# Inverse roots in the second edge stage: three Newton steps on VectorE in place of ScalarE's square root and a reciprocal

## What is computed

```
def _inst_norm_lastdim(t):
    mu = jnp.mean(t, axis=-1, keepdims=True)
    var = jnp.mean(jnp.square(t - mu), axis=-1, keepdims=True)
    return (t - mu) * jax.lax.rsqrt(var + EPS)
qkv = jnp.einsum('bnc,fc->bnf', x, Wqkv)        # 8 heads of 64
k = _inst_norm_lastdim(k)
v = _inst_norm_lastdim(v)
dots = jnp.einsum('bhnd,bhne->bhde', k, v)
out = jnp.einsum('bhnd,bhde->bhne', q, dots) / n
```

## Time and profile before

| | |
|---|---|
| median of 3 runs | 1760.73 us |
| lowest and highest | 1758.09 and 1762.08 us |
| the profiled execution | 1765.67 us, its span 1763.9 us |
| busy, share of the span | PE 77%, DVE 53%, POOL 54%, ACT 35% |
| TensorE's mean granted clock | 0.868 of full speed |
| second edge stage, first to last product | 798.2 to 1538.9 us |

### The profile page before, as it was taken

One profiled execution on the slowest core, in us unless ns is written; L12 is line 12 of the kernel. 1 busy time (PEld: TensorE's weight loads), 2 busy tenths in 40 slices (PEclk: granted clock), 3 DMA queues, 4 the chain that ended last, 5 costly groups with the idle time before them and its releaser, 6 DMA issues.

```text
span 1763.9 us, 39415 instructions
## 1 busy us (share of the span) xinstructions
PE 1350.7 (77%) x13431; PEld 801.7 (45%) x13431; DVE 935.0 (53%) x2353; ACT 616.5 (35%) x1897; POOL 957.8 (54%) x1008
## 2 busy tenths in 40 slices
PE   3668778877788775657778787888887878856999
PEld 1345454554455444343444444444444444543458
DVE  4445555454433343655555555555555556676763
ACT  2233333333333332243343433334343433323420
POOL 0677777777777774016665666666566656500000
PEclk9699988988988898778888888888888888977999
DMA  6333333333333330323333333333333333300001
GB/s 199 96 81 75 81 81 75 76 86 75 87 75 82 75 85 20 134 69 100 92 102 89 101 89 93 91 96 93 94 91 89 97 90 103 85 24 1 1 10 38
DMA packets 78954, 141.94 MB, mean 80 GB/s; under 512 B 25483, under 2 KB 34091, under 8 KB 78249
## 3 DMA queue, kind: packets, MB, share of 16 engines
q0 software_dynamic: 40128, 81.99, 17.8%
q1 hardware_dynamic: 38632, 57.46, 10.9%
HBM read 134.69 MB, written 4.67 MB: 79 GB/s over the span
## 4 chain that ended last, share of the span: by engine, by line
PE 44%; POOL 16%; issue 15%; DVE 12%; ACT 5%; DMA 5%; DVEq 2%; SPq 1%; ACTq 0%; POOLq 0%; PEldq 0%
POOL ring L412 16%; PE ps L932 8%; PE ps L946 8%; DVE arena L1357 5%; PE ps L919 5%; DMA ring<-mtab,src 4%; PE ps L968 4%; PE ps L1093 3%; PE ps L1084 3%; PE ps L762 2%; DVE arena L1355 2%; ACT wfT L583 1%; PE ps L694 1%; DVE arena L1347 1%; PE ps L775 1%
## 5 line engine op out<-in xcount | busy, mean ns | idle before, releaser
L422 POOL DMA_INDIRECT arena<-utab,src x500 | 473.3, 947 | 368.9 <-issue 143.5
L412 POOL DMA_INDIRECT ring<-mtab,src x500 | 482.3, 965 | 205.7 <-issue 197.2
L1223 DVE TENSOR_TENSOR arena<-ps,ring 128x1024 f32<-128x1024 f32 x125 | 153.0, 1224 | 290.7 <-PE ps L762 278.2
L932 PE MATMUL ps<-arena 64*128 64x256 f32 x1016 | 171.6, 464 | 144.7 <-DVE arena L1357 100.8
L571 ACT ACTIVATE arena<-ps 128x512 f32<-128x512 f32 x193 | 116.8, 605 | 360.0 <-PE ps L919 358.2
L1357 DVE TENSOR_TENSOR arena<-ps,arena 128x768 f32<-128x768 f32 x252 | 228.3, 948 | 0.0
L932 PEld LDWEIGHTS ps<-arena 64*128 64x128 f32 x1016 | 102.2, 216 | 184.1 <-DVE arena L1357 66.9
L946 PE MATMUL ps<-arena 128*8 128x256 f32 x4032 | 184.1, 330 | 0.0
L1347 DVE TENSOR_TENSOR arena<-arena,ps 128x16 f32 x512 | 87.3, 171 | 174.1 <-PE ps L955 116.8
L762 PE MATMUL ps<-arena,ring 128*64 128x128 f32 x2000 | 162.1, 313 | 0.0
L753 PE MATMUL ps<-ring 128*32 128x97 f32 x1000 | 49.3, 270 | 138.8 <-DMA ring<-mtab,src 136.4
(11 more groups left out here) (222 smaller groups left out, 1864.4 us busy)
## 6 DMA issues: line engine op xcount, KB each, us to landing
arena<-in_eaT SPq DMA_DIRECT2D x125, 256.0 KB
ring<-mtab,src POOLq DMA_INDIRECT x500
arena<-utab,src POOLq DMA_INDIRECT x500
arena<-in_rbf SPq DMA_DIRECT2D x132, 32.0 KB
ring<-in_fw SPq DMA_DIRECT2D x2, 1024.0 KB, 5.8
utab<-arena SPq DMA_DIRECT2D x1, 2048.0 KB, 7.5
XT<-in_xT SPq DMA_DIRECT2D x2, 1000.0 KB
arena<-in_x SPq DMA_DIRECT2D x1, 1920.0 KB, 9.5
```

Of the source, the lines that this page charges most:

```text
L412: pool.indirect_dma_start(MR[:, n % 4, k, 0:H], None, mtab, bass.IndirectOffsetOnAxis(ap=src[:, 4 * n + k:4 * n + k + 1], axis=0)).then_in ...
L422: pool.indirect_dma_start(G1[:, n % NSLOT, k, :], None, utab, bass.IndirectOffsetOnAxis(ap=src[:, 4 * n + k:4 * n + k + 1], axis=0)).then_ ...
L932: mm = pe.matmul(ps[:, 2 + h, a * D:(a + 1) * D], R3[hs, c:c + P], m4[hs, :], start=True, stop=True)
L1223: dve.tensor_tensor(RM[:, n % 2, :, :, :], ps[:, 1, 0:P].rearrange("p (t q) -> p t q", t=4).unsqueeze(3).broadcast_to([P, 4, KH, WIN]), SW ...
```

## The change

At f=4 and f=5 VectorE alone forms the inverse root. It reads the product of the two variances as an integer, shifts it right by one bit, and subtracts that from a constant (two instructions); this is a first guess. Three Newton steps follow, of three instructions each, one at f=4 and two at f=5. ScalarE's square root and VectorE's reciprocal are gone. Each of the new instructions waits for the one ahead of it through the semaphore `s_vnf`. The operands are 128 partitions x 8 numbers, as before; a new place in memory, `RK1`, holds the intermediate and the result. ScalarE's scaling at f=6 waits for the twelfth increment of the tile.

```diff
--- before.py
+++ after.py
@@ -71,6 +71,7 @@
 ARENA = 32256
 RING = 7744
 SEL = N // 2 - 1
+RSQ0 = 1597463040
 
 
 class Area:
@@ -218,6 +219,7 @@
         woT = arena[:, 30848:31872].rearrange("p (k c) -> p k c", k=4)
         mask64 = arena[:, 31872:32000]
         VS1 = arena[:, 32000:32016].rearrange("p (u h) -> p u h", u=2)
+        RK1 = arena[:, 32016:32032].rearrange("p (u h) -> p u h", u=2)
         KVM1 = arena[:, 30336:30848].rearrange("p (g c) -> p g c", g=4)
         K1 = [ring[:, 6720:7232], arena[:, 29824:30336]]
         VN1 = ring[:, 7232:7744]
@@ -276,7 +278,7 @@
             "s_e", "s_relu", "s_tr", "s_rc", "s_mask", "s_seg", "s_oc", "s_aff", "s_ae", "s_con", "s_conc",
             "s_rmw", "s_step", "s_base",
             "s_u", "s_ue", "s_o0", "s_w1", "s_ff", "s_up", "s_upr", "s_utab", "s_w4", "s_fw1",
-            "s_k1", "s_k1q", "s_v1", "s_v1q", "s_v1s", "s_v1std", "s_rk1", "s_v1n", "s_kvt1", "s_vnf",
+            "s_k1", "s_k1q", "s_v1", "s_v1q", "s_v1s", "s_v1n", "s_kvt1", "s_vnf",
             "s_kvm1", "s_A1", "s_Am1", "s_G1", "s_Gm1",
             "s_y1", "s_y1e", "s_acc1", "s_mlp", "s_silu", "s_tpw", "s_prod", "s_seg1", "s_ev", "s_turn", "s_rmw1", "s_oh",
             "s_ar", "s_are", "s_b", "s_bt", "s_bte", "s_o", "s_oe", "s_nr", "s_nre", "s_nvar", "s_nstd",
@@ -596,15 +598,12 @@
                 if t < NT and f == 3:
                     act.wait_ge(S["s_v1"], c + 1)
                     squares(1).then_inc(S["s_v1q"], 1)
-                if t < NT and f == 5:
-                    act.wait_ge(S["s_vnf"], c + 1)
-                    act.activation(VS1[:, 0, :], VS1[:, 0, :], ACT.Sqrt).then_inc(S["s_v1std"], 1)
                 if t < NT and f == 6:
-                    act.wait_ge(S["s_rk1"], c + 1)
+                    act.wait_ge(S["s_vnf"], 12 * c + 12)
                     act.wait_ge(S["s_kvt1"], c + 1)
                     for h in range(8):
                         v = act.activation(VN1[:, 64 * h:64 * h + 64], ps[:, 6, 64 * h:64 * h + 64], ACT.Identity,
-                                           scale=VS1[:, 0, h:h + 1])
+                                           scale=RK1[:, 1, h:h + 1])
                     v.then_inc(S["s_v1n"], 1)
                 if n == 7 * NT + 5:
                     act.wait_ge(S["s_A1"], j + 1)
@@ -1364,15 +1363,27 @@
 
                     t, f = divmod(n, 7)
                     c = j * NT + t
+                    xk, tk, yk = VS1[:, 0, :], RK1[:, 0, :], RK1[:, 1, :]
                     if t < NT and f == 4:
                         dve.wait_ge(S["s_v1q"], c + 1)
                         vs = VS1.rearrange("p u h -> p (u h)")
                         dve.tensor_scalar(vs, vs, 1.0 / 64, EPS, ALU.mult, ALU.add).then_inc(S["s_v1s"], 1)
                         dve.wait_ge(S["s_v1s"], c + 1)
-                        dve.tensor_tensor(VS1[:, 0, :], VS1[:, 0, :], VS1[:, 1, :], ALU.mult).then_inc(S["s_vnf"], 1)
-                    if t < NT and f == 5:
-                        dve.wait_ge(S["s_v1std"], c + 1)
-                        dve.reciprocal(VS1[:, 0, :], VS1[:, 0, :]).then_inc(S["s_rk1"], 1)
+                        dve.tensor_tensor(xk, xk, VS1[:, 1, :], ALU.mult).then_inc(S["s_vnf"], 1)
+                        dve.wait_ge(S["s_vnf"], 12 * c + 1)
+                        dve.tensor_scalar(yk.bitcast(I32), xk.bitcast(I32), 1, None,
+                                          ALU.arith_shift_right).then_inc(S["s_vnf"], 1)
+                        dve.wait_ge(S["s_vnf"], 12 * c + 2)
+                        dve.tensor_scalar(yk.bitcast(I32), yk.bitcast(I32), -1, RSQ0, ALU.mult,
+                                          ALU.add).then_inc(S["s_vnf"], 1)
+                    if t < NT and f in (4, 5):
+                        for i in ((0,), (1, 2))[f - 4]:
+                            dve.wait_ge(S["s_vnf"], 12 * c + 3 * i + 3)
+                            dve.tensor_tensor(tk, yk, yk, ALU.mult).then_inc(S["s_vnf"], 1)
+                            dve.wait_ge(S["s_vnf"], 12 * c + 3 * i + 4)
+                            dve.scalar_tensor_tensor(tk, tk, -0.5, xk, ALU.mult, ALU.mult).then_inc(S["s_vnf"], 1)
+                            dve.wait_ge(S["s_vnf"], 12 * c + 3 * i + 5)
+                            dve.scalar_tensor_tensor(yk, tk, 1.5, yk, ALU.add, ALU.mult).then_inc(S["s_vnf"], 1)
                     if n == 7 * NT + 3:
                         dve.wait_ge(S["s_kvt1"], (j + 1) * NT + 1)
                         dve.tensor_tensor(KVM1, ps[:, 7, :].rearrange("p (g c) -> p g c", g=4),
```

## The result

The changed kernel takes 1697.31 us (median of 4 runs, 1693.0 to 1703.26) against 1759.64 us for the kernel before (4 runs, 1758.09 to 1762.08): a ratio of 0.9652, with a 95% interval of 0.9628 to 0.9675. That is 62 us less.

The account below looks back on a forecast made before the run. No engine fills the span; VectorE's wait for ScalarE's root, once a tile, lies on the path of VectorE and TensorE. Direct -24 us and clock -16 us make -40, from 1760.73 to 1721 us, range 1700 to 1749.

Parts of the forecast that it names:

- direct gain of 24 us: Second edge stage: 64.5 us of wait and reciprocal go, 40 us of new VectorE instructions come.
- The place of the wait and its length: At f=5, VectorE waits for ScalarE's root once a tile: 61.3 us in 16 times, plus 3.2 us for the reciprocal.
- The chain, 0.23 us a link, 40 us: VectorE at f=4 and f=5: 176 new instructions, each waiting for the one ahead, at 0.23 us, 40 us (35 to 55).
- No cover for the links: The new VectorE instructions lengthen the steps in full: 1.15 us at f=4 and 1.4 us at f=5, nothing hidden.
- The clock, -16 us out of at most 33: TensorE's shorter stall at f=5 lets its clock fall less at f=6, f=0 and f=1: -16 us, ends 0 and 33.
- the ceiling of 33: Most the clock could give: 25 us at f=0 and f=1 behind even tiles, 8 us at f=6.
- the guess of half: Half of the clock's 33 us taken as gained, since the trace has no gap of 2.3 us at f=5.
- The gaps: TensorE's idle time: at f=5 from 4.93 to 2.3 us, at f=4 from 0.62 to about 1.8 us.
- GpSimd does not become the bound: Second edge stage: gathers at least 1.25 us apart need 630 us for 126 steps, against some 700 left.
- the clock stays up: Rival: TensorE's clock stays up through all tiles, -57 us, 1704 us, or 1699 with links at 0.20; chance 0.16.
- Slower: Rival: gaps at f=4 and f=5 bring TensorE to half clock there in every tile, +18 us, 1779 us; chance 0.06.
- The chain is dear: Rival: VectorE's new instructions cost 0.31 us each, no clock gain, -10 us, 1751 us; chance 0.08.

Follow-up runs that it names:

- e3: Kernel before, root and reciprocal kept, only ScalarE's root moved ahead in its order, before the copy of sums it waited behind: 1653.26 us, ratio 0.9399.
- e6: Changed kernel with a second chain of 11 small products a tile, result unused, 5 at f=4 and 6 at f=5: 1727.34 us.
- e8: Changed kernel run again, unaltered, beside later experiments: 1699.94 us, ratio 0.9640.
- e1: Kernel before with 13 zero-block matmuls a tile filling TensorE's idle time at f=5, wait for the root kept: 1731.28 us, ratio 0.9852.
- e7: Kernel before, root and reciprocal kept, with 11 unused chained products a tile, 5 at f=4 and 6 at f=5: 1766.65 us, ratio 1.0042.
- e2: Changed kernel with 6 zero-block matmuls a tile in TensorE's idle time at f=5: 1724.63 us, ratio 0.9795.

## Why the prediction was wrong in size

The prediction adds a direct gain of 24 us and 16 us from the clock. Measured by the medians, the whole is 62 us. The direct part is 31 us by the steps f=4 and f=5, which leaves 31 us for the clock (an estimate, since the steps are from profiled executions and the whole from medians).

- **The place of the wait and its length** (61.3 us and 3.2 for the reciprocal): right. The wait is gone and no other took its place; e3, which removes it by another way, confirms it.
- **The chain, 0.23 us a link, 40 us**: mis-sized. It is 0.20 to 0.21 in the timeline, 35 to 37 us in all. I had let the spacing of L1347's accumulations (0.31, two rows of address and register work each) weigh on it; the new links are like the pair at 906.55. By phase, f=4 grew by 1.01 us and f=5 shrank by 2.95, together -31 us where the prediction had -24.
- **No cover for the links**: right. Five of them cost 1.01 us at f=4, and e6 shows nothing hidden at f=4 or f=5.
- **The clock, -16 us out of at most 33**: this is the step that failed. It gave some 31 us by the medians. In the profiled executions f=6, f=0 and f=1 together lost 2.44 us a tile, 39 us, and in e8, the same kernel again, 1.58 us, 25 us. e1, with the wait untouched, gives 28 us by the clock alone.
- **Where the ceiling of 33 came from**: it is the mis-sized term. I compared the steps behind an even tile with those behind an odd one and took the odd ones (5.8 and 6.5 us) as the undisturbed length. But the f=0 step of the two had a fall of the clock in it too, at PEclk 0.54; undisturbed, the same f=0 takes 4.0 us (948.1 to 952.1). And the two kinds of step differ by themselves: at PEclk 1.00, in the changed kernel and e3, f=0 takes 4.1 us behind an odd tile and 5.4 behind an even one, f=1 mostly 6.2 to 6.6 and 5.7, and f=6 4.1. Against these lengths the kernel before loses some 4 us a tile at f=6, f=0 and f=1, about 60 us in all (an estimate from these steps). About half of it came back. That the guess of half fits this larger ceiling is luck, since no row gave a ground for it.
- **The gaps**: near what was forecast where the clock was up. The one behind f=4 is 1.7 to 2.0 us in even tiles (1.8 was forecast), the one behind f=5 is 2.1 in even tiles and 1.3 to 1.7 in odd ones (2.3 was forecast, from tile 2). Half clock does follow them in some tiles, so the first step of the next tile is still disturbed in part of the stage.
- **GpSimd does not become the bound**: right for the changed kernel. e3's stage of 636.5 us stands close to the 625 us that 500 gathers at 1.25 us need, and there they may be the next limit; that was not tried.
- **The rivals**: "the clock stays up", 1704 or 1699 us, came nearest in time, and the prediction gave it 0.16. Its mechanism did not come: the clock still falls in many tiles (PEclk of the stage 0.94), and its figure came near by chance, since the 33 us that it adds are too small a ceiling. "Slower", by half clock at f=4 and f=5, did not come: such falls do happen at f=5 (0.75 behind tile 2), but VectorE's rounds cover them there, as e6 shows. "The chain is dear", at 1751 us, lies outside the range of 1700 to 1749 that is said to take it in; nothing else hangs on that slip.
- **The Trainium skill's rule** (VectorE: DVE Perf Modes, The DRAIN you can't avoid), that a semaphore between chained instructions costs nothing extra: with the estimate of 166 ns a link from its formula, it gave a direct sum of -35. The trace does not agree at this size. The same product on 128x8 numbers starts 0.20 us behind the one it waits for, and 0.09 us behind one that it does not wait for (e6, 900.79 to 900.88; it is 0.08 to 0.10 at f=4 of e7 too, behind a product). So a link cost some 0.11 us more than an instruction without the wait. That instruction also needs nothing from the one ahead; no run has a dependent one without the wait.

By phase, the profiled stage sums to -31 (wait less chain) and -39 (clock), -70 together, against 68.5 measured; in e8 it is -31 and -25, against 56.

## What to carry to other kernels

When an engine waits for a small result, look first at what stands ahead of the producer in its own queue: here a square root had its operand 6.6 us early (906.92, and it started at 913.52 with its table load) and stood behind a copy that waited for the current step. Moving that one instruction was worth 106 us, where rewriting the arithmetic for another engine was worth 62. A stall of TensorE is to be priced with the steps behind it: compare each with the same step at PEclk 1.00, not with the better of two disturbed ones and not with a step that has other work. And table loads are free where nobody waits for what stands behind them: in e3 all 32 are there, one of the two in each tile delays an activation, and the kernel is the fastest of all.

## What the runs showed of the hardware beyond that

- Integer shift, integer multiply-add, product and three-operand product on 128x8 mostly take 0.17 us on VectorE (means: 0.21 for the shift, 0.19 for the integer multiply-add, 0.17 for the others). They follow each other at 0.20 us in most cases and 0.21 in the mean, with a wait for the one ahead; without that wait the product followed at 0.09 us (e6).
- Filling TensorE's idle time with matmuls that add zeros kept the granted clock at its upper level for more of the stage (PEclk 0.97 in e1 against 0.87) and saved 28 us, 1.5%, of the kernel before. The weights were all zeros; no run used others. Where the filling outlasted the gap, the loss was larger than the gain (e2, 25 us slower).
- A table load took 1.28 us, and the activation behind it started 1.29 to 1.30 us after the load's start (913.52 to 914.81; in e3 894.04 to 895.34).
- The kernel before varied by 0.6% over all its runs (1756.3 to 1766.3 us), the changed one by 0.7% (1693.0 to 1704.9), and its f=0 and f=1 steps differ from one profiled execution to the next (5.34 and 6.59 us, then 5.67 and 7.18) while f=2 to f=5 agree within 0.02 us.
